# Expert 0's first six weight blocks split in the first phase, and half of its token facts multiplied on GpSimd

## The reference

```python
mod = (_silu(L0_c) @ L0_wmod).reshape(L0_c.shape[0], 6, 1, -1)
h = _layernorm(x, axis=-1) * (1 + ca) + sa
x = x + ga * _L0_attn_ref(h, L0_attn_W_qkv, L0_attn_W_out)   # linear attention, 16 heads of 16
h = _layernorm(x, axis=-1) * (1 + cb) + sb
x = x + gb * _L0_ffn_ref(h, L0_ffn_router_w, L0_ffn_wg, L0_ffn_wu, L0_ffn_wd)
```

## Time and profile before

| | us |
|---|---|
| median of 3 runs | 622.04 (619.25 to 622.12) |
| profiled execution, its own time | 624.11 |
| its span, first to last instruction | 622.4 |
| TensorE busy | 583.3 (94%) |
| VectorE busy | 452.6 (73%) |
| ScalarE busy | 320.8 (52%) |
| GpSimd busy | 269.1 (43%) |
| mean granted TensorE clock | 0.992 |

### The profile page before, as it was taken

How to read it: one execution, slowest core, us unless ns; L and a number is a source line. 1 busy time by engine, 2 the same in 40 slices (tenths; PEclk the granted TensorE clock), 3 DMA queues, 4 the chain that set the end, 5 groups by cost and what they waited for, 6 DMA issues and landing times.

```text
span 622.4 us, 13153 instructions
## 1 busy us (share of the span) xinstructions
PE 583.3 (94%) x4013; PEld 526.4 (85%) x4013; DVE 452.6 (73%) x1357; ACT 320.8 (52%) x718; POOL 269.1 (43%) x406
## 2 busy tenths in 40 slices
PE   6999999999999878899999999999999999999993
PEld 5587789898787333699999999999999999999993
DVE  4688899998899888786767667766676776566441
ACT  4688888886444333344445445445444454354331
POOL 5788857776688301302080170260350440612322
PEclk9999999999999899999999999999999999999997
DMA  6322468644666640517267067175273373450312
GB/s 174 103 68 78 116 190 247 213 145 131 198 198 188 209 121 0 151 39 218 72 119 198 23 122 206 35 139 156 62 152 116 87 144 103 103 127 8 35 19 25
DMA packets 92481, 75.29 MB, mean 121 GB/s; under 512 B 12156, under 2 KB 89094, under 8 KB 92424
## 3 DMA queue, kind: packets, MB, share of 16 engines
q1 hardware_dynamic: 82344, 57.39, 30.8%
q0 software_dynamic: 8992, 15.90, 13.7%
q10 hardware_dynamic: 1088, 1.31, 0.6%
HBM read 52.41 MB, written 22.16 MB: 120 GB/s over the span
## 4 chain that ended last, share of the span: by engine, by line
PE 59%; issue 9%; DVE 8%; DMA 3%; POOL 3%; ACT 2%; SPq 2%; POOLq 0%; ACTq 0%; DVEq 0%
PE bank L1684 28%; PE bank L1696 13%; PE bank L1717 4%; PE bank L1557 3%; DVE hit L1097 2%; PE bank L1732 2%; PE bank L1432 2%; DMA x_in<-x 1%; POOL xg L556 1%; PE bank L1635 1%; DMA q_in<-q_store 1%; PE bank L1543 1%; SPq L377 1%; PE bank L1616 1%; PE bank L1469 1%
## 5 line engine op out<-in xcount | busy, mean ns | idle before, releaser
L556 POOL DMA_INDIRECT xg<-h_rows,g_idx x40 | 43.2, 1081 | 235.6 <-DVE g_idx L1223 225.8
L1684 PE MATMUL bank<-xT_h,w_h 128*128 128x320 f32 x432 | 134.8, 312 | 1.2 <-DVE hid L1309 0.8
L1684 PE MATMUL bank<-xT_l,w_h 128*128 128x320 f32 x432 | 133.1, 308 | 0.0
L1684 PE MATMUL bank<-xT_h,w_l 128*128 128x320 f32 x432 | 132.9, 308 | 0.0
L755 ACT CAST hid_h<-hid 128x320 fp32r<-128x320 f32 x108 | 49.7, 460 | 85.9 <-DVE hid L1309 80.5
L566 POOL DMA_INDIRECT out<-yo,s_idx x40 | 66.6, 1666 | 62.1 <-DVE yo L1371 26.6
L752 ACT ACTIVATE act_g<-bank 128x320 f32<-128x320 f32 x108 | 47.2, 437 | 70.4 <-PE bank L1684 61.6
L1684 PEld LDWEIGHTS bank<-xT_h,w_h 128*128 128x128 f32 x432 | 81.1, 188 | 2.1 <-DVE hid L1309 1.0
L1684 PEld LDWEIGHTS bank<-xT_l,w_h 128*128 128x128 f32 x432 | 81.1, 188 | 0.0
L1684 PEld LDWEIGHTS bank<-xT_h,w_l 128*128 128x128 f32 x432 | 81.0, 188 | 0.0
L1696 PE MATMUL bank<-w_h,hid_h 128*128 128x256 f32 x280 | 80.2, 286 | 0.9 <-issue 0.5
(11 more groups left out here) (235 smaller groups left out, 1364.5 us busy)
## 6 DMA issues: line engine op xcount, KB each, us to landing
w_raw<-wg SPq DMA_DIRECT2D x32, 256.0 KB, 3.3
w_raw<-wu SPq DMA_DIRECT2D x32, 256.0 KB, 4.8
w_raw<-wd SPq DMA_DIRECT2D x16, 512.0 KB, 6.0
x_in<-x SPq DMA_DIRECT2D x32, 128.0 KB, 2.2
q_store<-qT SPq DMA_DIRECT2D x32, 128.0 KB, 2.2
q_in<-q_store SPq DMA_DIRECT2D x32, 128.0 KB, 2.3
x_re<-x SPq DMA_DIRECT2D x32, 128.0 KB, 2.2
out<-x SPq DMA_DIRECT2D x32, 128.0 KB, 2.2
```

The costliest lines, as they stand in the source:

```text
L556: nc.gpsimd.indirect_dma_start(out=xg[par][:, a, :], out_offset=None, in_=h2_rows, in_offset=bass.IndirectOffsetOnAxis(ap=g_idx[par][:, a: ...
L1684: last = MM(bank[2 * h + m][:, 0:HCAP], W[i][:, f, at:at + P], XT[j][:, k, cols], start=n == 0, stop=n == 3 * KC - 1)
```

## The change

Three things move. SP loads expert 0's weights in steps 2 to 11, one part a step, in place of steps 19 to 23. The first six blocks are split in halves of 384 columns: ScalarE writes one high half at the end of each of the steps 8 to 19 (`early_high`), VectorE one low half in each of the steps 9 to 20 (`early_low`), between `finish_stats` and `feat`; the splits of these six blocks behind the first stage are gone. And the second half of `facts` of expert 0 is multiplied by GpSimd, which waits for `in_block`; TensorE's `look(0)` waits for it ahead of its second half.

```diff
+EARLY, FIRST_SPLIT = 6, 8
...
-                if 0 <= s.rep - (LAG + 1) < WEIGHT_LOADS:
-                    part = s.rep - (LAG + 1)
-                    load_weights(0, 0, raw_a, parts=(part,))
-                    load_weights(0, FC // 2, raw_b, parts=(part,))
+                if 2 <= s.rep < 2 + 2 * WEIGHT_LOADS:
+                    part = (s.rep - 2) % WEIGHT_LOADS
+                    if s.rep < 2 + WEIGHT_LOADS:
+                        load_weights(0, 0, raw_a, parts=(part,))
+                    else:
+                        load_weights(0, FC // 2, raw_b, parts=(part,))
...
+            second = slice(NT // 2, NT)
+            pool.wait_ge(in_d, 1)
+            nc.gpsimd.tensor_tensor(facts[:, second, :, :], vals[:, second, :].unsqueeze(3).to_broadcast([P, NT // 2, NV, BLOCKS]),
+                                    in_block[:, second, :].unsqueeze(2).to_broadcast([P, NT // 2, NV, BLOCKS]), ALU.mult)\
+                .then_inc(half_d, 1)
...
+            def early_high(i):
+
+                f, cols = i // 2, slice(i % 2 * WU // 2, (i % 2 + 1) * WU // 2)
+                act.wait_ge(raw_a if f < FC // 2 else raw_b, WEIGHT_LOADS * 16)
+                nc.scalar.copy(w_h[:, f, cols], w_raw[:, f, cols]).then_inc(sp_h if i % 2 else half_h, 1)
...
+                if 0 <= s.rep - FIRST_SPLIT < 2 * EARLY:
+                    early_high(s.rep - FIRST_SPLIT)
...
-            for f in range(FC - 2):
-                split_high(0, f, f)
...
+            def early_low(i):
+
+                f, cols = i // 2, slice(i % 2 * WU // 2, (i % 2 + 1) * WU // 2)
+                dve.wait_ge(sp_h if i % 2 else half_h, f + 1)
+                ins = V.tensor_tensor(w_l[:, f, cols], w_raw[:, f, cols], w_h[:, f, cols].bitcast(F32), ALU.subtract)
+                if i % 2:
+                    ins.then_inc(sp_l, 1)
...
+                if 0 <= s.rep - FIRST_SPLIT - 1 < 2 * EARLY:
+                    early_low(s.rep - FIRST_SPLIT - 1)
...
-            describe(0)
+            describe_blocks(0)
+            describe_facts(0, 0)
+            describe_rows(0, 0)
+            describe_rows(0, 1)
             find_diagonal(0)
             find_tokens(0, 0)
             place_masks(1)
-            for f in range(4):
-                split_low(0, f, f)
             place_counts(1)
...
-            split_low(0, 4, 4)
...
-            split_low(0, 5, 5)
...
+                        if first and n:
+                            pe.wait_ge(half_d, 1)
```

More of the change, by code:

```diff
@@ L341, in build_program @@
         band_d, diag_d, place_d, spot_d = (sem(n) for n in ("band_d", "diag_d", "place_d", "spot_d"))
-        facts_d, look_d, idx_d = (sem(n) for n in ("facts_d", "look_d", "idx_d"))
+        facts_d, look_d, idx_d, half_d = (sem(n) for n in ("facts_d", "look_d", "idx_d", "half_d"))
         raw_a, raw_b, sp_h, sp_l = (sem(n) for n in ("raw_a", "raw_b", "sp_h", "sp_l"))
+        half_h = sem("half_h")
         ga_d = [sem(f"ga_d{g}") for g in range(XG)]
@@ L1198, in describe_rows @@
                    row_in[:, sl].unsqueeze(2).to_broadcast([P, NT // 2, ROWS]), ALU.is_equal).then_inc(facts_d, 1)
[L1200 to L1204, removed]
             def find_diagonal(e):
@@ L1609, in _, with look @@
             count_masks(0)
-            def look(e):
+            def look(e, first=False):
                 for n in range(0, NT, Q):
@@ L1638, in _ @@
             keep_on(6, 17)
-            look(0)
+            look(0, first=True)
             keep_on(6, 3)
```

## The result

The changed kernel takes 630.27 us (median of 5 runs, 629.62 to 631.71), the kernel before 622.04 beside it (5 runs, 619.25 to 623.54). The ratio is 1.0136, with an interval of 1.0116 to 1.0156. A second series gave 630.71 against 622.09 and 1.0146 (1.0114 to 1.0178). So the change costs 8 to 9 us. I had forecast 629.7, 7.7 us more than before.

A forecast was written before the change was run, and what follows sets the result against it. In the first phase's 3.42 us step, a ring, no engine has 0.6 us to spare, and delays ahead of expert 0 reach the end. Terms 5.8 + 2.8 - 0.3 + 0.7 - 1.2 - 0.1 = +7.7 on 622.04: 629.7 us, range 621.8 to 633.0.

The forecast's parts named there:

- low halves, steps 9 to 15: First phase: each low half waits behind GpSimd's rot, making steps 4.42 or 4.02 us instead of 3.42; +5.8 us.
- low halves, steps 16 to 20: First phase: feat starts 1.79 us after rot in these steps, where VectorE makes hT_l itself; +5.0 us before slack.
- taken up by TensorE's slack: Steps 16 to 20: rot_b ends 2.2 us before TensorE's product that waits for it, absorbing that much, leaving +2.8.
- loads: Weights loaded in steps 2 to 11 instead of 19 to 23 no longer delay x_in; -0.3 us, between -0.6 and 0.
- facts: Behind the routing: GpSimd's half runs in turn with VectorE's facts and onehots; +0.7 us, between -0.74 and +0.9.
- gathers: Ahead of expert 0: without four low products two gathers shorten by some 0.6 us each; -1.2 us, between 0 and -1.7.
- fifth and sixth block: Beside TensorE's opening of expert 0: their casts and products are gone from there; -0.1 us.
- Mechanism A: First phase: low halves held by GpSimd products make the kernel slower, 627 to 633 us; chance 0.66.
- High halves at cost 0: Steps 8 to 19: ScalarE's casts fit in 0.51 us of idle time; cost 0, at most 0.5 a step otherwise.
- Rival B: First phase: low halves slip in unheld at their own length, price 1.2 instead of 8.6, so 622.3 us; chance 0.22.
- C: Faster: low halves vanish in gaps, facts run side by side (-0.74), gathers give 1.7; about 619.1 us; chance 0.06.
- D: First phase: x_in loads between weights take longer than a step, +3 us, 632.7 with Mechanism A; chance 0.06.

The follow-up runs named there:

- experiment 5: Kernel before with only expert 0's weight loads moved to steps 2 to 11; ratio to the kernel before 1.0000.
- experiment 2: Changed kernel with one input of the low halves of steps 9 to 18 read from PSUM instead of SBUF; ratio to the kernel before 1.0054.
- experiment 9: Kernel before with early loads and, in steps 9 to 18, a 128x384 VectorE product of two SBUF inputs ahead of feat; ratio 1.0104.
- experiment 10: Kernel before with early loads and, in steps 9 to 18, a 128x384 VectorE product ahead of feat, second input from PSUM; ratio 0.9979.
- experiment 3: Changed kernel with the low half moved from behind finish_stats to between rot_a and the first rot_b; ratio to the kernel before 1.0051.
- experiment 4: Changed kernel without early low halves and GpSimd's half of the facts, keeping ScalarE's high halves and early loads; ratio to the kernel before 1.0030.
- experiment 6: Kernel before with only the second half of expert 0's facts moved to GpSimd; ratio to the kernel before 1.0013.
- experiment 7: Kernel before with six high blocks on ScalarE in steps 40 to 45, their low products on GpSimd at the search's start; ratio 1.0166.
- experiment 8: Kernel before with high blocks on ScalarE in steps 40 to 45, low products as twelve GpSimd halves, each timed behind beats of a search round; ratio 1.0033.
- experiment 11: Changed kernel with high halves in steps 20 to 31, low halves on GpSimd timed in the search, facts on VectorE; ratio to the kernel before 0.9973.

## Right or wrong, step by step

| step | foretold | measured |
|---|---|---|
| low halves, steps 9 to 15 | +5.8 | +5.85 |
| low halves, steps 16 to 20 | +5.0 | +5.0 |
| taken up by TensorE's slack | -2.2 | -0.5 |
| loads | -0.3 | -0.8 |
| facts | +0.7 | +0.3 |
| gathers | -1.2 | -0.8 |
| fifth and sixth block | -0.1 | -0.2 |
| sum | +7.7 | +8.9 (+9.5 at the first product) |

The measured entries are differences of marks of the two first traces, with two exceptions. The loads are from experiment 5. The fifth and sixth block, which stand behind the first product, are the experts' 362.9 us in the second trace of before against 362.7 and 362.65 after the change; one trace of before cannot show so small a difference. Some 0.5 us between step 26 and the routing have no owner; traces of the same kernel differ there by that and more.

*Mechanism A was right, its place and its size too.* Low halves of 1.46 us against my 1.3 to 1.5, steps of 4.43 and 3.97 against 4.42 and 4.02. Experiments 2, 9 and 10 show that the second SBUF input is what makes them wait, experiment 3 that the place does. The objection that no row had shown a wait as long as 0.9 us did not hold: what was left of one of 1.29 us, 0.9 us, is waited out whole. The Trainium skill, page "SBUF — State Buffer", section "Who interferes with whom", says so too: whoever issues first has the shared pair for the whole instruction, and a VectorE instruction with at most one SBUF input is outside of it, unless it runs in one of the modes that use both ports. The 1.46 and 0.55 us agree.

*High halves at cost 0: right as a sum, wrong as a reason.* I took 0.51 us of idle ScalarE for room. Experiment 4 shows that the cast costs 0.4 us a step, 2.4 over steps 9 to 15. In the changed kernel that is hidden, because VectorE's held step is the longer ring (4.43 against 3.82; experiment 9 has the same 30.2 us without any cast). My text did put the cost at up to 0.5 a step if the cover were gone.

*TensorE's slack: the step that failed.* I saw rot_b end 2.2 us ahead of the product that waits for it and took these as time to catch up. Of the 10.8 us lost by step 20, feat of step 26 has got back 1.3, and the loads are 0.8 of it. TensorE's busy time from step 20 on, before and after (order of columns as in the earlier trace rows):

```profile
92.40:124.33 31.93, 31.74 (x219) 28.56 (x217) 29.78 (x124) 26.57 (x67) 24.36 (x42) 1.00 0.74 226
```

```profile
103.15:133.75 30.60, 28.97 (x200) 25.97 (x199) 29.46 (x123) 24.54 (x61) 23.09 (x41) 1.00 0.46 143
```

Before, TensorE had been busy for 31.74 of 31.93 us: nothing can be caught up in a stretch that an engine fills, except by what it has done ahead. That was something: TensorE had started 482 matmuls by feat of step 20 in place of 468, and 2.8 us less work is left behind it. But it now stands for 1.6 us in the stretch, waiting for attT and feat, so that the stretch is only 1.3 us shorter. The 2.2 us that rot_b's reader waited were mostly TensorE's queue, and only to a small part a reserve.

*Rival B*: not the case; its price of 1.2 was even too high. *C*: the facts do not run beside one another (experiment 6). *D*: not the case. Feat of step 8 is at 48.09 (48.18 before), and in steps 9 to 26 VectorE waits for no load of x_in; before it did twice, for 0.37 us at 66.52 and for 0.80 at 116.53. Two sums of the rivals were loose: C's terms make -2.8 and not -2.9, and D's three or four steps of 1.1 us make 3.4 to 4.5 and not 3. Neither touches the forecast.

*Facts and gathers*: both right in sign. GpSimd's half takes 1.2 us of its own, not 1.6. The gathers became as short as foretold (0.95), but tile 2 landed somewhat later behind its issue: TensorE still waits 0.58 us for it. The alternative by the Trainium skill (same page and section, where it is called inferred), that the low products would not hold up a gather, is refuted: with VectorE's low products behind `g_idx` the second gather took 1.67 to 1.69 us in each of the traces, and without them 0.96, in experiments 7, 8 and 11 as in the changed kernel. The rows also show what is held, and it is the start alone. In the first trace of before the second gather is issued at 248.65, a low product ends at 249.49, and the gather ends at 250.32: the 0.95 us of a free gather begin at 249.37, 0.12 us before the product's end. The third is issued at 250.63 and ends at 252.05, so its 0.95 us begin at 251.10. These are the products beside them:

```profile
249.41 0.95 DVE L1238 TENSOR_TENSOR w_l<-w_raw,w_h 128x768 fp32r<-128x768 f32 x1
...
250.27 0.95 DVE L1238 TENSOR_TENSOR w_l<-w_raw,w_h 128x768 fp32r<-128x768 f32 x1
```

The one of 249.41 runs at its own length beside the rest of the second gather, and the one of 250.27 holds the third until 0.13 us before its end, much as rot does the low halves. Whether it is the gather's reading of `g_idx` that waits at its start or something else is not shown.

*Against the clock*: 9.5 us at the first product between the first traces and 8.6 between the second, 8.2 and 8.6 between the medians. My 7.7 came that near because the errors were small beside the term that was right, and in part by luck: the slack was out by 1.7 us, and the loads and the facts, each out by 0.4 to 0.5 the other way, took half of it back.

## What to carry to other kernels

Before putting a VectorE product with two SBUF inputs into a step, look at what GpSimd runs at the very moment of its issue: the price is what is left of that operation, and it is paid both ways. An idle share of an engine is no room by itself. Look at what ends the gap: ScalarE's gaps in experiments 4 and 8 were ended by TensorE's answer to ScalarE's own output, and they moved along with whatever was put in. Where another engine fills the step (experiment 11) the gap was room, and so was VectorE's gap ahead of feat (experiment 10). In both cases the remedy was another place for the same work (experiment 11).

## What the runs showed of the hardware

Some VectorE operations with a single SBUF tensor are held by GpSimd too. In experiment 7 cand (a tensor_scalar of 3 columns, which also reads won, one value a partition) took 1.15 us in place of 0.23, and the cast val 0.59 in place of 0.29, while hit, which writes an accumulator as well, stayed at 0.48. Not all of the kind are: nm and ve, tensor_scalars of one column, take 0.15 and 0.14 us in the middle of rot (55.51 in the rows at the top). The Trainium skill, same page and section, lists tensor_scalar and cast as able to take the shared pair, on conditions for their operands, and excepts the form with the accumulator; the rows agree with both, and what sets nm and ve apart from cand is not shown. In the same experiment TensorE was busy for only 1.1 us from 214 to 218, and the granted clock then was 0.50, the lower of its two levels, from 217 to 219 and again from 225 to 237. Before, it was 1.00 from the start of the search on.

ScalarE's stand of 5.1 us, once in the experts, is in eleven of the fourteen traces, and the experts then take 365.4 to 367.1 us in place of 362.6 to 362.9. The first trace of the kernel before, ScalarE:

```profile
538.30 0.83 ACT L706 CAST w_h<-w_raw 128x768 fp32r<-128x768 f32 x1
544.27 0.44 ACT L752 ACTIVATE act_g<-bank 128x320 f32<-128x320 f32 x1 [5.13 <-remote]
```

No releaser in the program is named for it. Both traces of the changed kernel are without it, and one of two of the kernel before, so whether the change had a part in that stays open. It is worth more than any single term here but the first two, and it was not tried on its own.
